# A two-layer graph network: layer 0's output split as rows and transposed by one DMA per tile, two weight loads issued from ScalarE's queue

## What is computed

```python
# layer 0: 2 relations, hidden width F = 286
h   = x * rsqrt(mean(x**2) + 1e-6) * ln_weight
out = h @ W_root + bias + sum_r (segment_sum(h[src] @ W_rel[r] * (type2 == r), dst) / max(count_r, 1))
y   = elu(out)                       # 625 x 286
x1  = layernorm(2 * x + y @ wo)      # wo is 286 x 1024
# layer 1: 8 relations, width 1024
u   = x1 @ root + b + sum_r ((segment_sum(x1[src] * (type8 == r), dst) / max(count_r, 1)) @ weight[r])
z   = concat([u, x1]) @ w_gate + b_gate
res = layernorm(x1 + tanh(u) * z + x1 * (1 - z))
```

## Time and profile before

| | us |
|---|---|
| median of 3 runs | 844.56 (844.36 to 845.41) |
| the profiled execution | 845.03 |
| its span, first to last instruction | 843.2 |
| TensorE busy | 814.7 (97%) |
| VectorE busy | 672.1 (80%) |
| ScalarE busy | 442.6 (52%) |
| granted TensorE clock, mean | 0.994 |

### The profile page before, as it was taken

One profiled execution on the slowest core, in us unless ns is written; L12 is line 12 of the kernel. 1 busy time (PEld: TensorE's weight loads), 2 busy tenths in 40 slices (PEclk: granted clock), 3 DMA queues, 4 the chain that ended last, 5 costly groups with the idle time before them and its releaser, 6 DMA issues.

```text
span 843.2 us, 15807 instructions
## 1 busy us (share of the span) xinstructions
PE 814.7 (97%) x6276; PEld 580.5 (69%) x6276; DVE 672.1 (80%) x972; ACT 442.6 (52%) x614; POOL 14.1 (2%) x32
## 2 busy tenths in 40 slices
PE   3989999999999999999999999999999999999996
PEld 2556754458867768678687686876867868678543
DVE  8889698989987677787776867767777786788996
ACT  6788676556565353562544535545355354545711
POOL 1000000000000000000000000000000000000000
PEclk9899999999999999999999999999999999999999
DMA  9200368402220211202202022021120220306811
GB/s 312 65 2 1 127 224 176 150 1 100 101 101 1 101 56 46 99 0 99 96 3 99 1 98 99 0 99 37 62 99 0 99 81 21 125 1 151 200 50 73
DMA packets 51676, 68.72 MB, mean 81 GB/s; under 512 B 22214, under 2 KB 25922, under 8 KB 51635
## 3 DMA queue, kind: packets, MB, share of 16 engines
q1 hardware_dynamic: 50759, 67.30, 24.7%
q10 hardware_dynamic: 876, 0.85, 0.4%
HBM read 57.71 MB, written 5.18 MB: 75 GB/s over the span
## 4 chain that ended last, share of the span: by engine, by line
PE 88%; DVE 6%; ACT 3%; DMA 1%; issue 1%; SPq 0%; DVEq 0%; ACTq 0%
PE psP L1151 50%; PE psA L1222 20%; PE psP L974 12%; PE psA L963 3%; ACT cu_mem L664 2%; PE psP L1082 1%; PE psP L934 1%; DVE xT L1374 1%; DMA stage<-in_L_gnn_W_root 1%; DVE wsplit L1395 0%; DMA xT<-cu_mem 0%; DVE p_mem L1448 0%; DVE p_mem L1447 0%; DVE am L1494 0%; DVE wsplit L1360 0%
## 5 line engine op out<-in xcount | busy, mean ns | idle before, releaser
L1151 PE MATMUL psP<-wsplit,xT 128*128 128x256 f16 x2592 | 294.6, 273 | 0.0
L1151 PEld LDWEIGHTS psP<-wsplit,xT 128*128 128x128 f16 x2592 | 253.5, 98 | 33.1
L1222 PE MATMUL psA<-p_mem,cu_mem 128*128 128x512 f16 x800 | 175.3, 379 | 0.0
L1151 PE MATMUL psP<-wsplit,x 128*128 128x256 f16 x1296 | 150.3, 273 | 0.0
L1222 PEld LDWEIGHTS psA<-p_mem,cu_mem 128*128 (+1 forms) x800 | 78.3, 98 | 91.0 <-DVE cu_mem L1703 0.3
L1151 PEld LDWEIGHTS psP<-wsplit,x 128*128 128x128 f16 x1296 | 126.8, 98 | 14.7
L1409 DVE SCALAR_TENSOR_TENSOR wsplit<-stage,sc,wsplit 128x1024 f16<-128x1024 f32 x90 | 114.8, 1279 | 26.8 <-ACT wsplit L659 26.8
L659 ACT ACTIVATE wsplit<-stage,sc 128x1024 f16<-128x1024 f32 x90 | 100.6, 1137 | 16.6 <-DVE sc L1291 10.6
L1703 DVE SCALAR_TENSOR_TENSOR cu_mem<-psA,coef,cu_mem 128x512 f32<-128x512 f32 x80 | 60.0, 750 | 31.4 <-PE psA L1222 30.0
L659 ACT ACTIVATE wsplit<-x,sc 128x1024 f16<-128x1024 f32 x54 | 61.7, 1143 | 41.7 <-PE psP L1151 31.1
L638 ACT ACTIVATE dump<-stage 128x1024 f16<-128x1024 f32 x72 | 75.8, 1053 | 3.8 <-DMA stage<-in_L_gnn_weight 2.1
(11 more groups left out here) (209 smaller groups left out, 785.6 us busy)
## 6 DMA issues: line engine op xcount, KB each, us to landing
stage<-in_L_gnn_weight SPq DMA_DIRECT2D x16, 2048.0 KB, 7.7
stage<-in_L_gnn_w_gate SPq DMA_DIRECT2D x4, 2048.0 KB, 7.7
x_home<-x SPq DMA_DIRECT2D x5, 512.0 KB, 3.5
x<-x_home SPq DMA_DIRECT2D x5, 512.0 KB, 5.5
x<-in_x SPq DMA_DIRECT2D x4, 512.0 KB, 8.2
xT<-in_L_gnn_root SPq DMA_DIRECT2D x1, 2048.0 KB, 8.9
stage<-in_L_gnn_root SPq DMA_DIRECT2D x1, 2048.0 KB, 7.9
out<-x SPq DMA_DIRECT2D x4, 512.0 KB
```

The costliest lines, as they stand in the source:

```text
L1151: last = nc.tensor.matmul(psP[:, bank, (col + tt) * FB:(col + tt + 1) * FB], lhs[tt](a, c), split_block(n, b)[:, c, :], start=(first and t ...
L1222: last = nc.tensor.matmul(psA[:, (NT * h + t) % 2, :], cnt8[:, r, s, t * P:(t + 1) * P], p_part[h][a][:, s, :], start=(s == 0 and a == 0), ...
```

## The change

Steps 3 and 4 change places. `y_high` and `y_low` read `acc0` as it stands (rows of nodes) and write both parts side by side into `y_rows`, a new view of the end of `p_mem`. One DMA transpose a tile, of 128 x 768, then writes both parts into `yT`. The 15 transposes on TensorE are gone. `wo_product(t)` waits for the tile's transpose, and `x1_high` for `y_lo` instead of `y_turned`. SP issues these five transposes where the two loads stood; ScalarE issues the loads (`early_load`), between its own instructions and with the same waits. The order on ScalarE, VectorE and TensorE changes with that; `degrees8(5, 7)` moves ahead of `wo_product(2)`.

```diff
+        y_rows = p_mem[:, 2 * NT * HALF - FC * NPAD:2 * NT * HALF].bitcast(F16).rearrange("p (t a f) -> p t a f", t=NT, a=2)
-        y_turned = sem("y_turned")
+        yT_ready = [sem(f"yT_ready{t}") for t in range(NT)]
# SP
-            sp.wait_ge(wo_lo, 1)
-            load(U_ROOT + 1, 1, by_chunk(root_d[:, HALF:D]))
-            sp.wait_ge(agg0_full, NT * R0)
-            w1_v = w1_d.rearrange("r (c p) f -> p (r c) f", p=P)
-            sp.wait_ge(wsum_ready, 5)
-            load(U_REL, 0, w1_v[:, 0:DC, 0:HALF])
+            def turn_y(t):
+                sp.wait_ge(y_lo, t + 1)
+                sp.dma_start_transpose(yT[:, :, :, t * P:(t + 1) * P].rearrange("p a c n -> p (a c) n"),
+                                       y_rows[:, NT - 1 - t, :, :].rearrange("p a f -> p (a f)")).then_inc(yT_ready[t], 16)
+            turn_y(0)
+            turn_y(1)
+            for t in range(2, NT):
+                turn_y(t)
# ScalarE
+            def early_load(slot, v):
+                act.dma_start(stage[:, slot, :].rearrange("p (c f) -> p c f", c=DC), by_chunk(v)).then_inc(stage_full[slot], 16)
             def y_high(t):
-                act.wait_ge(y_turned, t + 1)
-                nc.scalar.activation(yT[:, 0, :, t * P:(t + 1) * P],
-                                     psA[:, t % 2, 0:FPAD].rearrange("p (c n) -> p c n", c=FC), ACT.Copy).then_inc(y_hi, 1)
-            for t in range(NT - 1):
-                elu_exponential(t)
+                act.wait_ge(y_ready, t + 1)
+                nc.scalar.activation(y_rows[:, NT - 1 - t, 0, :], acc0[:, t, :], ACT.Copy).then_inc(y_hi, 1)
+            elu_exponential(0)
+            elu_exponential(1)
             y_high(0)
             y_high(1)
+            elu_exponential(2)
+            elu_exponential(3)
             weight_sum(U_ROOT, 0, slot_load(U_ROOT), parts=(0, 1))
+            act.wait_ge(wo_lo, 1)
+            early_load(1, root_d[:, HALF:D])
             elu_exponential(NT - 1)
             weight_sum(U_ROOT, 0, slot_load(U_ROOT), parts=(2, 3))
-            y_high(2)
-            y_high(3)
+            act.wait_ge(agg0_full, NT * R0)
+            act.wait_ge(wsum_ready, 5)
+            early_load(0, w1_d[0, :, 0:HALF])
+            for t in range(2, NT):
+                y_high(t)
             raw_high(U_ROOT, 0)
-            y_high(4)
# TensorE
-            def turn_y(t):
-                ...
             def wo_product(t):
...
-                pe.wait_ge(y_hi, t + 1)
-                pe.wait_ge(y_lo, t + 1)
+                pe.wait_ge(yT_ready[t], 16)
...
             aggregate0(NT - 2)
-            turn_y(0)
-            turn_y(1)
             aggregate0(NT - 1)
             degrees8(2, 5)
             wo_product(0)
-            turn_y(2)
-            turn_y(3)
             wo_product(1)
-            turn_y(4)
+            degrees8(5, 7)
             wo_product(2)
             wo_product(3)
-            degrees8(5, 7)
             wo_product(4)
# VectorE
             def y_low(t):
                 dve.wait_ge(y_hi, t + 1)
-                tt(yT[:, 1, :, t * P:(t + 1) * P], psA[:, t % 2, 0:FPAD].rearrange("p (c n) -> p c n", c=FC),
-                   yT[:, 0, :, t * P:(t + 1) * P], ALU.subtract).then_inc(y_lo, 1)
+                tt(y_rows[:, NT - 1 - t, 1, :], acc0[:, t, :], y_rows[:, NT - 1 - t, 0, :], ALU.subtract).then_inc(y_lo, 1)
             elu_end(0, 2)
             agg0_add(2)
+            y_low(0)
+            y_low(1)
             agg0_add(3)
             wo_low()
-            y_low(0)
-            y_low(1)
             agg0_add(4)
             elu_end(2, NT)
+            for t in range(2, NT):
+                y_low(t)
             unit_scale(U_ROOT, 0)
-            y_low(2)
-            y_low(3)
...
             raw_low(U_ROOT, 0, (0, 1))
             x1_factors(0)
-            y_low(4)
             wo_add(1, 0)
```

More of the change, by code:

```diff
@@ L515, in _ @@
                     sp.dma_start_transpose(xT[:, a, :, t * P:(t + 1) * P], x1_rows[:, t, a, :]).then_inc(x1T_ready[t], 16)
+            w1_v = w1_d.rearrange("r (c p) f -> p (r c) f", p=P)
             sp.wait_ge(wlo_ready, weight_blocks(U_REL))
@@ L773, in x1_high @@
             def x1_high(t):
-                act.wait_ge(y_turned, NT)
+                act.wait_ge(y_lo, NT)
                 act.wait_ge(x1_ready, t + 1)
@@ L1085, in aggregate0 @@
                     last.then_inc(agg0_full, 1)
-            def turn_y(t):
-                pe.wait_ge(y_ready, t + 1)
-                if t >= 2:
-                    pe.wait_ge(y_lo, t - 1)
-                for c in range(FC):
-                    last = nc.tensor.transpose(psA[:, t % 2, c * P:(c + 1) * P], acc0[:, t, c * P:(c + 1) * P], ident[:, :])
-                last.then_inc(y_turned, 1)
             def wo_product(t):
```

## The result

The changed kernel took 849.66 us, median of 4 runs (849.02 to 850.46), against 844.85 us for the kernel before in the same session (844.36 to 845.41): a ratio of 1.0056, 95% interval 1.0042 to 1.0070. It is slower by 4.8 us, outside the range that was given. The profiled executions say the same: 849.23 us against 845.03, span 847.4 us against 843.2, mean granted clock 0.993 against 0.994.

A forecast was written before the change was run, and what follows sets the result against it. It took the path to the first root product to be bound by VectorE, ScalarE and x1's transpose, not TensorE. Terms 0.0 + 0.3 + 0.0 + 0.0 = +0.3 us gave 845.3 profiled, forecast 844.9; range 843.7 to 849.3.

The forecast's parts named there:

- yardstick: Start of the first root product on TensorE, 135.17 us before the change; everything behind it was to move with it.
- VectorE's steps: VectorE's reordered work up to the first `wo_add`, which was to come at 116.65 against 116.85: -0.2 us.
- The late scale: ScalarE's `raw_high` of the root waits for VectorE's later `unit_scale`, starting +0.8 us late; +0.3 us on the path.
- The issues on ScalarE at 0: Two early loads issued on ScalarE, taken as 0.45 us each, hidden in its waits; from 0 to +0.3, taken as 0.
- TensorE's saved transposes at 0: 15 transposes and a wait, 2.6 us of TensorE time, all ahead of 134.5; worth 0 on the path.
- With half of the engines' time while the loads last it lands at 120.5: Tile 2's y transpose, sharing the DMA engines with the loads, was to land at 120.5; undisturbed at 118.3.
- the end of the cover (123.1): Latest landing of tile 2's transpose at which TensorE's 12.4 us of work still ends by the root product at 135.5.
- 0.0 (transposes, while covered): Term of the sum for the y transposes on SP: they add 0.0 us while tile 2 lands before 123.1.
- late transposes: Rival: y transposes starve until both loads are through, tile 2 lands at 125.9; 847.7, or 850.4 with half clock; chance 0.33.
- most of the load is gone by 118: Argument against y's transposes being held up by the two 2 MB loads, given beside the 4.8 us of slack.
- cover of 4.8 us: Slack for tile 2's transpose, between its undisturbed landing at 118.3 and 123.1, when TensorE would become late.

The follow-up runs named there:

- c_before_act: Kernel before, with plain copies for its DMA transposes and its two early loads issued from ScalarE; 844.65 us, ratio 0.9990 to the kernel before.
- e_split: Changed kernel, with plain copies for its DMA transposes and the second early load placed behind `raw_high` in ScalarE's program; 846.38 us, ratio 1.0006 to the kernel before.
- c_sp_fifo: Changed kernel with plain copies for DMA transposes, both early loads on SP ahead of the copies of tiles 2 to 4; 850.89 us, ratio 1.0059.
- copy_after: Changed kernel with every DMA transpose replaced by a plain copy of the same bytes in 256-byte runs; 849.42 us, ratio 1.0052 to the kernel before.
- c_long_runs: Changed kernel with plain copies for DMA transposes, y's in one run of 1536 bytes a partition instead of six of 256; 846.09 us, ratio 1.0008.
- e_after_yhigh: Changed kernel with plain copies for DMA transposes, second early load placed behind `y_high(4)` in ScalarE's program; 849.66 us, ratio 1.0041 to the kernel before.

## Why the prediction was wrong

**Right.** That the first root product is the yardstick: +4.17 of +4.20 us. VectorE's steps: `wo_add` at 116.48 (predicted 116.6), root's `raw_high` at 116.60 (116.7), the table load at 120.88 (121.0). The late scale: x1's transposes were issued 36.24 us behind `wo_high` against 35.76 before, +0.5 us where +0.3 was summed. The issues on ScalarE at 0: *c_before_act*. TensorE's saved transposes at 0: after removing everything else, D is still 40.75 against 40.19.

**The step that failed** is "With half of the engines' time while the loads last it lands at 120.5". It landed at 124.95, past the end of the cover (123.1), at the time of the load's own landing (125.2), so the term written as "0.0 (transposes, while covered)" was the whole +4.2 us. Two rows were read a little short (36 matmuls as 7.8 us for 7.93, 50 columns as 1.3 for 1.39), which changes nothing. The rival *late transposes* had the mechanism in the main (y did move packets beside the load, from 118.9 us on, but too few), and its two ends hold the result: it gave 847.7 with the clock at full and 850.4 at half. Its parts were each a little large: the landing was 1.0 us earlier than its 125.9, and the clock took 13.49 - 11.81 = 1.7 us for the 54 matmuls, not 2.7, as half of the stretch at half clock had passed before they began.

**Why half was wrong.** I took the share of the engines to be split evenly from the moment of issue, and nothing in the trace of before had a small DMA beside a load of another queue. The runs show that the place in the order of issue decides. Issued ahead of the load, in pieces of 256 bytes, tile 2 lands in 4.4 us (*e_split*); issued 0.4 to 1.9 us behind it, in 9.1 to 10.4 us, with two queues or with one. The part that the forecast had at nothing is the time ahead of the first packet: 3.98 us in the kernel after, 1.25 to 1.32 us where no load had been issued just ahead.

The Trainium skill (DMA: Bandwidth & Descriptors, "Queues, rings and completion order") has the engines take turns between queues packet by packet. Read as equal time from the issue on, that gave 120.5; the measured 124.95 decides against this reading. Once y moves, the trace agrees with turns by packet (306 for 310 of the load in 119 to 121 us of *copy_after*), and such turns give a queue of 256-byte packets far less than half beside one of 2 KB packets; *c_long_runs* has the same 3.94 us ahead of its first packet and is 3 us faster behind it. The Trainium skill's other rule that I leaned on ("Issuing engines are not separate DMA queues": another issuing engine brings no bandwidth) agrees with *c_sp_fifo*.

What holds the other queue's first packet back for 4 us is open, and so is why the landing comes 1.8 us later behind the last packet. Inside a single queue it is the order of the packets (*c_sp_fifo*). The statement against the rival, "most of the load is gone by 118", was true of the first load only, which landed at 118.4 in the kernel after; the second landed at 124.4 in the earlier trace rows itself.

**The chance** given to the rival, 0.33, was too low for what stood in the earlier trace rows: engines 0.87 busy, a load of 10.5 us issued just ahead of the need. The forecast's cover of 4.8 us was counted from the undisturbed landing, at a time when nothing was undisturbed.

## What to carry to other kernels

In these runs a small DMA in 256-byte pieces, issued just behind a 2 MB load, landed with that load, whichever queue the load was in: issue the load behind the small ones, and not so late that it meets the next small one. Where the order can't be changed, longer pieces help (3.3 us of 5.2 here). When TensorE's work is moved to the DMA engines, price its landing at the landing of the load ahead of it first, and add TensorE's half clock for what follows the wait. Check in the trace when a DMA in ScalarE's program is really issued, as the program's order doesn't say it.

## What the runs showed of the hardware

- ScalarE issues a DMA ahead of the end of the activations that stand before it: 116.30 us, 0.06 us into the first of four `raw_high` (*e_split*), and at 114.07, 0.22 us before `y_high(4)`, behind which it stands, had begun (*e_after_yhigh*). So the sentence of the first section, that each engine executes its own instructions in order, does not hold between ScalarE's activations and the DMAs in its program.
- A copy issued behind a fresh 2 MB load of the other queue moved its first packet 3.9 to 4.2 us after its issue (seven runs), otherwise 1.25 to 1.32 us after it (eight runs).
- An issue on SP itself can stall beside a load: 3.30 us for tile 3's transpose in the kernel after, three issues in 6.41 us in *e_after_yhigh* against 2.03 us in *e_split*.
- Half clock lasted some 6.8 us in the kernel after (121.7 to 128.5 us), as long as at 23 us in the earlier trace rows, and 10.2 us in *e_after_yhigh* (119.3 to 129.6 us). It can come after waits of 1 to 2 us too (*e_split*).
- The times of the packets that started in 123 to 125 us add up to 1.25 of the 16 engines' time, for 81 GB/s, most of it y's 256-byte packets. A sum above 1 means that packets' times overlap, so this column is not a share of what the engines could do.
